# Hybrid conv, attention and MLP kernel: the token layer norms cut into four slices

## The chip, the cores and the metric

One core of a Trainium2 chip runs the whole kernel. The metric is the device time of one execution in microseconds (us), as the median of several runs.

## The reference, cut to what matters

The whole model has a Mamba stage over an image, a group norm with three depthwise convolutions, and then, for each of 4 batches of 4096 tokens with 96 channels, two layers of attention and MLP. The change lies in that last part alone:

```python
def _ln_t(v, eps=1e-5):
    m = jnp.mean(v, axis=-1, keepdims=True)
    s = jnp.var(v, axis=-1, keepdims=True)
    return (v - m) / jnp.sqrt(s + eps)
...
x = x + _L1_conv_ref(_gn(x), ...)
t = _to_tokens(x)
t = t + _L2_attn_ref(_ln_t(t), ...)      # linear attention, no softmax
t = t + _L2_ffn_ref(_ln_t(t), ...)       # 96 -> 384 -> 96, relu, fp8 products
t = t + _L3_attn_ref(_ln_t(t), ...)
t = t + _L3_ffn_ref(_ln_t(t), ...)
x = _from_tokens(t, x)
```

Every token's 96 values are normalised before each of the four blocks of a batch, 16 times in all over a tile of 4096 tokens.

## The kernel before, in words

The first 3.57 ms (the Mamba stage, the group norm and the depthwise convolutions) are not touched. What follows is `batch_phase`'s last block, from 3569 us of the span to its end at 4346 us.

Tokens stand as 32 tiles of 128 tokens on the 128 partitions with 96 values each, so that a whole batch is 3072 elements a partition. A **chunk** is 4 tiles (512 tokens); a phase has 8 chunks. The prologue fuses the convolution outputs of batches 0 and 1 in 8 **groups** of 1024 tokens: TensorE multiplies (`fuse`, L1253), VectorE adds the residual (`add_input`, L1511), TensorE transposes (`turn_rows`, L1262), ScalarE copies to `t_next` (`rows`, L1391). The groups of batches 2 and 3 are fused one or two at a time at the start of phases 1 to 7 (`FUSE_PHASE`); finished batches are transposed and stored ahead of phases 8 and 9 and after phase 15 (`turn_out`, L1350).

There are 16 **phases**, numbered p: attention of batch 0, attention of batch 1, MLP of batch 0, MLP of batch 1, the same for layer 2, and then all of it for batches 2 and 3. So phases 0, 1, 4, 5, 8, 9, 12 and 13 are attention, and 2, 3, 6, 7, 10, 11, 14 and 15 are MLP. The layer norm of phase p+1 is computed during phase p; that can be done because it needs the output of phase p-1. Each engine has its program in a fixed, hand-written order, and semaphores count what is done.

One **layer norm** is this chain. VectorE `center`: a sum over the 96 channels (L1487), a small multiply by 1/96 (L1488), a subtraction into `dev` (L1489). ScalarE `squares` (L1378): `dev` squared into `haug`. VectorE `variance`: a sum (L1495) and a small multiply-add (L1496). ScalarE `roots` (L1383). VectorE `scale`: a small reciprocal (L1501) and the product of `dev` and the reciprocal into `haug` (L1502). Each is one instruction over all 32 tiles. TensorE waits for the whole norm before its phase (`ln_ready`, p + 1).

An **attention phase**: TensorE transposes each chunk of `haug` (`turn`, L1272; ScalarE copies it to `h_t`, L1398) and adds its Gram matrix (L1286); when all 8 chunks are in, four small products follow one another (L1297), each with a VectorE instruction behind it (L1523 to L1531, the first being the copy of the Gram matrix); then the output products chunk by chunk (L1306), each added to the residual by VectorE (L1539). The two-slot PSUM tile `tp` holds transposes and outputs, so TensorE can be two chunks ahead of who empties them. VectorE's order is: `center`, `add_input` where a group is due, `variance`, the five Gram steps, `scale`, eight residual additions. ScalarE's is: `h_t` copies of chunks 0 to 5, `squares`, copies 6 and 7, `roots`.

An **MLP phase**, for each chunk and three thirds: TensorE multiplies (L1337), ScalarE evicts to `hid16` (L1431, four slots), VectorE adds a bias with relu (L1556) and casts to fp8 (L1550), TensorE multiplies back (L1320), ScalarE copies out (L1419), and GpSimd adds the bias (L1596) and then adds to the residual (L1599). VectorE does `center` after chunk 1, `variance` after chunk 4, `scale` after chunk 6; ScalarE does `squares` after chunk 3 and `roots` after chunk 5.

In the prologue VectorE does `center(0)` after group 3, `variance(0)` after group 4, `scale(0)` after group 5, and ScalarE does `squares(0)` and `roots(0)` between the copies of groups 3 and 4.

Of the kernel before, what the change touches and what calls it, by code (L numbers as in the profile page):

```python
# [11 lines left out]
ALU = mybir.AluOpType  # L12
# [830 lines left out]
CONV_GROUPS = 4  # L843
# [18 lines left out]
def batch_phase(nc, dram, f_dram, x0_dram, x_stats, f_stats, out):  # L862
# [4 lines left out]
    with ExitStack() as ctx:  # L867
# [352 lines left out]
        with nc.Block() as block:  # L1220
# [23 lines left out]
            def _(pe):  # L1244
# [21 lines left out]
                def turn(p, c, kind, rows):  # L1266

                    fill = fills[kind, p, c]
                    if fill >= 2:
                        pe.wait_ge(t_taken, fill - 1)  # L1270
                    for j in range(4):
                        last = pe.transpose(tp[0:rows, fill % 2, j * TILE:(j + 1) * TILE], haug[:, p % 2, 4 * c + j, 0:rows],  # L1272
                                            ident[:, :])
                    last.then_inc(t_full, 1)

                def attention(p):
                    n, layer = nth(p), phase_of(p)[1]
                    pe.wait_ge(ln_ready, p + 1)
                    pe.wait_ge(t_taken, fills[ATT_T, p, 0])
# [30 lines left out]
                def mlp(p):  # L1310
# [13 lines left out]

                    pe.wait_ge(ln_ready, p + 1)
                    pe.wait_ge(t_taken, fills[MLP_T, p, 0])
# [47 lines left out]
            def _(act):  # L1374
                def squares(v):

                    act.wait_ge(ln_centered, v + 1)
                    act.activation(haug[:, v % 2, :, 0:C], dev[:, :, :], ACT.Square).then_inc(ln_squared, 1)  # L1378

                def roots(v):  # L1380

                    act.wait_ge(ln_var, v + 1)
                    act.activation(stat[:, 2, :], stat[:, 1, :], ACT.Sqrt).then_inc(ln_root, 1)  # L1383

# [9 lines left out]
                def attention(p):  # L1394
                    for c in range(CHUNKS):
                        fill = fills[ATT_T, p, c]
                        act.wait_ge(t_full, fill + 1)
                        act.activation(h_t[:, c * CHUNK:(c + 1) * CHUNK], tp[0:C + 1, fill % 2, :],  # L1398
                                       ACT.Copy).then_inc(t_taken, 1)
                        if p + 1 < PHASES and c == SQUARE_AFTER[0]:  # L1400
                            squares(p + 1)
                    if p + 1 < PHASES:
                        roots(p + 1)

                def mlp(p):
# [17 lines left out]
                    for c in range(CHUNKS):  # L1423
# [8 lines left out]
                        if c > 0:  # L1432
                            add_up(c - 1)
                        if p + 1 < PHASES and c == SQUARE_AFTER[1]:
                            squares(p + 1)
                        if p + 1 < PHASES and c == ROOT_AFTER:
                            roots(p + 1)
                    add_up(CHUNKS - 1)
# [12 lines left out]
                squares(0)  # L1451
                roots(0)
                for i in range(CONV_GROUPS, first):
                    rows(i)
                for p in range(PHASES):
# [12 lines left out]
            def _(dve):  # L1468
# [7 lines left out]

                def center(v):

                    b, layer, is_mlp = phase_of(v)
                    src = residual_of(v)  # L1480
# [6 lines left out]
                    chain(dve.tensor_reduce(stat[:, 0, :], src, AXIS.X, ALU.add))  # L1487
                    chain(dve.tensor_scalar(stat[:, 0, :], stat[:, 0, :], 1.0 / C, None, ALU.mult))  # L1488
                    dve.tensor_tensor(dev[:, :, :], src, stat[:, 0, :].unsqueeze(2).to_broadcast([128, TILES, C]),  # L1489
                                      ALU.subtract).then_inc(ln_centered, 1)  # L1490

                def variance(v):

                    dve.wait_ge(ln_squared, v + 1)
                    chain(dve.tensor_reduce(stat[:, 1, :], haug[:, v % 2, :, 0:C], AXIS.X, ALU.add))  # L1495
                    dve.tensor_scalar(stat[:, 1, :], stat[:, 1, :], 1.0 / C, LN_EPS, ALU.mult, ALU.add).then_inc(ln_var, 1)  # L1496

                def scale(v):

                    dve.wait_ge(ln_root, v + 1)  # L1500
                    chain(dve.reciprocal(stat[:, 2, :], stat[:, 2, :]))  # L1501
                    dve.tensor_tensor(haug[:, v % 2, :, 0:C], dev[:, :, :], stat[:, 2, :].unsqueeze(2).to_broadcast([128, TILES, C]),  # L1502
                                      ALU.mult).then_inc(ln_ready, 1)

# [9 lines left out]
                def attention(p):  # L1514
                    n, (b, layer, _) = nth(p), phase_of(p)
                    if p + 1 < PHASES:
                        center(p + 1)
                    for i in due(FUSE_PHASE, p):
                        add_input(2 * CONV_GROUPS + i)
                    if p + 1 < PHASES:  # L1520
                        variance(p + 1)
                    dve.wait_ge(gram_full, n + 1)
# [8 lines left out]
                    dve.tensor_tensor(gram[:, 0, 0:C], mp[0:C + 1, 0, 0:C], bff[:, layer, :], ALU.add).then_inc(gram_step, 1)  # L1531
                    if p + 1 < PHASES:
                        scale(p + 1)
                    src = residual_of(p)
                    for c in range(CHUNKS):
# [3 lines left out]
                        dve.tensor_tensor(t[:, b % 2, tiles, :].rearrange("p j c -> p (j c)"), tp[:, fill % 2, 0:4 * C],  # L1539
                                          src[:, tiles, :].rearrange("p j c -> p (j c)"), ALU.add).then_inc(t_taken, 1)  # L1540

                def mlp(p):
# [9 lines left out]
                    for c in range(CHUNKS):  # L1552
# [20 lines left out]
                for i in range(CONV_GROUPS):  # L1573
# [126 lines left out]
```

## Time and profile before

| what | value |
|---|---|
| runs | 4346.25, 4350.67, 4351.54 us; median 4350.67 |
| profiled execution | 4347.45 us, of which the span of its instructions is 4345.6 us |
| mean granted TensorE clock | 0.918 of full speed |
| whole span, busy | TensorE 85%, VectorE 77%, GpSimd 66%, ScalarE 55% |
| prologue and phases | 3569 to 4346 us: 777 us, of which TensorE 527.5, VectorE 444.0, ScalarE 282.4, GpSimd 155.5 us busy |
| an attention phase | 33 to 47 us, by what is fused or stored in front of it |
| an MLP phase | 43 to 50 us; the last one, which has no layer norm to compute, 29 us |

The profile is one execution on the chip. A timeline row gives the start, the duration, the engine and line, the operation, the tiles with their sizes (partitions x elements), how many instructions the row holds, and in square brackets the idle time of that engine just before it and who ended it. "PE" is TensorE, "DVE" VectorE, "ACT" ScalarE, "POOL" GpSimd.

### The profile page before, as it was taken

To read this page: it belongs to the slowest core of one execution; us is meant where nothing else is said; L and a number is where in the kernel's file an instruction comes from. 1 tells how busy PE (TensorE), PEld (TensorE's weight loads), DVE (VectorE), ACT (ScalarE), POOL (GpSimd) and SP (SyncE) were. 2 spreads that over 40 slices of the span, in tenths; PEclk is the share of its full clock that TensorE was granted. 3 is DMA by queue.
4 is the path that set the end of the run, shared out by engine and by line. 5 is a ranking of instruction groups with operands and counts; after the bars stand their busy time and mean duration, and the time that the engine had idled before them with its cause. 6 is when DMAs were issued, how large, how long until landed. Compare 5 with 4: busy or idle time off the path is not lost. (4 is left out here: it accounts for less than half of the span.)

```text
span 4345.6 us, 39976 instructions
## 1 busy us (share of the span) xinstructions
PE 3674.2 (85%) x11136; PEld 1703.6 (39%) x11136; DVE 3347.4 (77%) x3962; ACT 2373.1 (55%) x3961; POOL 2852.7 (66%) x2326
## 2 busy tenths in 40 slices
PE   6899999999999999999999999987129988685766
PEld 2333333333333333333333333332029985463554
DVE  4999999999999999999999999999320004656565
ACT  5667666667666667666667666665121101425334
POOL 4988999988999988999988999988100000203123
PEclk8999999999999999999999999999569998777666
DMA  3555555555555555555555555555564456100000
GB/s 89 180 160 166 164 166 162 175 169 165 164 165 162 177 168 164 168 161 162 178 168 163 168 162 163 175 160 170 134 163 145 147 146 154 31 15 15 15 1 29
DMA packets 246461, 607.50 MB, mean 140 GB/s; under 512 B 56496, under 2 KB 90419, under 8 KB 245087
## 3 DMA queue, kind: packets, MB, share of 16 engines
q1 hardware_dynamic: 210654, 535.73, 41.9%
q10 hardware_dynamic: 35584, 69.23, 5.7%
q8 instruction: 89, 1.46, 0.1%
q14 instruction: 134, 1.09, 0.1%
HBM read 553.77 MB, written 72.56 MB: 144 GB/s over the span
## 5 line engine op out<-in xcount | busy, mean ns | idle before, releaser
L785 POOL TENSOR_TENSOR prod<-states,c_rows 128x512 f32<-128x512 f32 x1536 | 1922.7, 1272 | 176.9 <-DVE states L715 142.7
L715 DVE TENSOR_TENSOR_SCAN states<-decay,carry,bpsum 128x512 f32<-128x512 f32 x1344 | 1677.2, 1259 | 0.0
L444 PE MATMUL ypsum<-prod,identity 128*128 128x512 f32 x3072 | 1593.7, 602 | 0.5 <-POOL prod L785 0.3
L550 ACT ACTIVATE decay<-delta,decay_rate 128x512 f32<-128x512 f32 x1344 | 934.7, 711 | 312.5 <-DVE states L715 308.2
L695 DVE TENSOR_TENSOR bpsum<-bpsum,dx 128x512 f32<-128x512 f32 x1344 | 904.6, 673 | 138.5 <-PE bpsum L437 124.3
L1596 POOL TENSOR_TENSOR y<-y,b 128x384 f16<-128x384 f16 x64 | 66.4, 1038 | 1072.3 <-ACT y L1419 1072.3
L444 PEld LDWEIGHTS ypsum<-prod,identity 128*128 128x128 f32 x3072 | 583.3, 194 | 422.4 <-issue 283.4
L437 PE MATMUL bpsum<-b_rows,select 96*128 96x512 bf16 x1344 | 522.0, 389 | 211.8 <-DVE states L715 209.3
L437 PEld LDWEIGHTS bpsum<-b_rows,select 96*128 96x128 bf16 x1344 | 129.4, 96 | 974.3 <-DVE states L715 690.7
L1020 PE MATMUL convp<-image,band_w 128*128 128x252 f32 (+3 forms) x1440 | 334.2, 395 | 19.2 <-DMA image<-normed_map 19.2
L1020 PEld LDWEIGHTS convp<-image,band_w 128*128 128x128 f32 x1440 | 332.7, 325 | 20.4 <-issue 19.2
L550 ACT ACTIVATE bpsum<-delta,decay_rate 128x512 f32<-128x512 f32 x192 | 132.6, 691 | 309.6 <-DVE states L715 308.7
L1572 DVE MEMSET haug<- 128x64 f32 x1 | 0.1, 112 | 356.6 <-PEq L1151 356.6
L484 PE MATMUL mm<-h_norm,w_xs 96*128 96x512 f32 x512 | 262.7, 599 | 6.0 <-ACT h_norm L616 6.0
L492 PE MATMUL mm<-h_norm,w_xs 96*64 96x512 f32 x512 | 267.5, 616 | 0.0
L813 POOL TENSOR_TENSOR drive<-b_wide,dx 128x512 f32<-128x512 f32 x192 | 243.9, 1270 | 30.1 <-DMA b_wide<-bc_map 28.5
L715 DVE TENSOR_TENSOR_SCAN states<-bpsum,carry,drive 128x512 f32<-128x512 f32 x192 | 243.7, 1269 | 0.9 <-issue 0.9
L626 ACT ACTIVATE xpre<-mm,cols 128x512 f32<-128x512 f32 x96 | 65.7, 684 | 301.2 <-PE mm L492 168.6
L794 POOL TENSOR_TENSOR tmp<-zpre,tmp 128x512 f32<-128x512 f32 x96 | 122.3, 1274 | 130.3 <-ACT zpre L595 130.3
L1064 ACT ACTIVATE dw_sums<-convp 128x768 f32<-128x768 f32 x48 | 38.9, 811 | 307.4 <-PE convp L1020 307.4
L1556 DVE TENSOR_SCALAR hid<-hid,b 128x512 f16<-128x512 f16 x192 | 90.3, 488 | 88.7 <-ACT hid L1431 84.3
L484 PEld LDWEIGHTS mm<-h_norm,w_xs 96*128 96x128 f32 x512 | 97.9, 192 | 132.3 <-issue 123.7
(184 smaller groups left out, 4486.3 us busy)
## 6 DMA issues: line engine op xcount, KB each, us to landing
c_rows<-bc_map SPq DMA_DIRECT2D x512, 512.0 KB, 3.9
c_rows<-bc_map SPq DMA_DIRECT2D x512, 256.0 KB, 4.1
b_wide<-bc_map ACTq DMA_DIRECT2D x128, 256.0 KB, 4.7
band_rows<-tap_bands SPq DMA_DIRECT2D x64, 360.0 KB, 5.6
band_w<-band_rows SPq DMA_DIRECT2D x96, 240.0 KB, 3.9
depthwise_map<-dw_sums ACTq DMA_DIRECT2D x48, 384.0 KB, 4.4
dw_parts<-depthwise_map SPq DMA_DIRECT2D x16, 1152.0 KB, 7.7
b_wide<-bc_map ACTq DMA_DIRECT2D x128, 128.0 KB, 4.2
```

Source lines behind the costliest of these rows:

```text
L437: pe.matmul(bpsum[:, n % B_BANKS, :], pick, b_rows[k % 2][:, :], start=True, stop=True).then_inc(b_full, 1)
L444: pe.matmul(ypsum[:, group % Y_BANKS, :], identity[:, :], prod[:, n % P_RING, :], start=s == 0, stop=s == STATES - 1).then_inc(summed, 1)
L484: last = pe.matmul(mm[:, b, :], w_xs[:, layer, k, 0:128], h_norm[:, b, k:k + CHUNK], start=k == 0, stop=k == TAPS - 1)
L492: last = pe.matmul(mm[b * HALF:b * HALF + HALF, 0, :], w_xs[:, layer, k, 128:DIN], h_norm[:, b, k:k + CHUNK], start=k == 0, stop=k == TAPS ...
L550: act.activation(into, delta[k % 2][:, g, :], ACT.Exp, scale=decay_rate[:, ORDER[k][0], g, s:s + 1]).then_inc(done, 1)
L695: dve.tensor_tensor(bpsum[:, n % B_BANKS, :], bpsum[:, n % B_BANKS, :], dx[k % 2][:, g, :], ALU.mult).then_inc(scaled, 1)
L715: dve.tensor_tensor_scan(states[:, n % H_RING, :], by, add, carry[:, at, u:u + 1], ALU.mult, ALU.add).then_inc(scanned, 1)
L785: pool.tensor_tensor(prod[:, n % P_RING, :], states[:, n % H_RING, :], c_rows[:, n // C_STATES % C_RING, n % C_STATES, :], ALU.mult).then_ ...
L794: pool.tensor_tensor(tmp1[:, g, :], zpre[:, g, :], tmp1[:, g, :], ALU.subtract).then_inc(lost_ready, 1)
L813: pool.tensor_tensor(drive[:, i % B_RING, :], b_wide[:, i % B_RING, :], dx[k % 2][:, g, :], ALU.mult).then_inc(driven, 1)
L1020: last = pe.matmul(into[:, :, left:right], bands[:, p % W_RING, :, TAP_AT[k] + kx], image[:, p % I_RING, :, left + kx - pad:right + kx - pad],
L1556: dve.tensor_scalar(hid16[:, i % 4, :], hid16[:, i % 4, :], b1[:, layer, k:k + 1], 0.0, ALU.add, ALU.max).then_inc(hid_relu, 1)
```

## The change

Each norm is cut into `SLICES` = 4 slices of 8 tiles (768 elements a partition), and every step of the chain is issued once for a slice. The semaphores count slices (`SLICES * v + k + 1`), also where TensorE waits: `turn` of chunk c waits for slice c // 2 alone. `center` waits for the two chunks (or the one group) that its slice reads, and no more for all of them.

- Prologue: `center(0, k)` stands after group k + 2, `variance(0, k)` after k + 4, `scale(0, k)` after k + 5; ScalarE squares after copies 3 to 6 and takes roots after copies 4 to 7.
- Attention: VectorE does four `center` slices, `add_input`, four `variance` slices, the Gram steps, and `scale(k)` behind the residual additions 1, 3, 5 and 7. ScalarE does `squares(k)` behind the `h_t` copies 1, 3, 5 and 7, and the four roots at the end.
- MLP: `center(k)` after chunk k, `squares(k)` in chunk k + 1, `variance(k)` after chunk k + 2, `roots(k)` in chunk k + 3, `scale(k)` after chunk k + 4.

```diff
-SQUARE_AFTER, ROOT_AFTER = (5, 3), 5
-CENTER_AFTER, VARIANCE_AFTER, SCALE_AFTER = 1, 4, 6
+SLICES = 4
+ATT_SQUARE, ATT_SCALE = (1, 3, 5, 7), (1, 3, 5, 7)
+MLP_CENTER, MLP_SQUARE, MLP_VARIANCE, MLP_ROOT, MLP_SCALE = range(5)
+SLICE = TILES // SLICES
...
                 def turn(p, c, kind, rows):
+                    pe.wait_ge(ln_ready, SLICES * p + c * SLICES // CHUNKS + 1)
...
-                    pe.wait_ge(ln_ready, p + 1)
...
-                def squares(v):
-                    act.wait_ge(ln_centered, v + 1)
-                    act.activation(haug[:, v % 2, :, 0:C], dev[:, :, :], ACT.Square).then_inc(ln_squared, 1)
+                def squares(v, k):
+                    act.wait_ge(ln_centered, SLICES * v + k + 1)
+                    tiles = slice(SLICE * k, SLICE * (k + 1))
+                    act.activation(haug[:, v % 2, tiles, 0:C], dev[:, tiles, :], ACT.Square).then_inc(ln_squared, 1)
...
                 def center(v, k):
                     b, layer, is_mlp = phase_of(v)
+                    tiles = slice(SLICE * k, SLICE * (k + 1))
                     if layer == 0 and not is_mlp:
-                        dve.wait_ge(rows_taken, CONV_GROUPS * (b + 1))
+                        dve.wait_ge(rows_taken, CONV_GROUPS * b + k + 1)
                     elif not is_mlp:
-                        dve.wait_ge(t_step, CHUNKS * (nth(v - 2) + 1))
+                        dve.wait_ge(t_step, CHUNKS * nth(v - 2) + CHUNKS // SLICES * (k + 1))
                     else:
-                        dve.wait_ge(t_taken, fills[ATT_O, v - 2, CHUNKS - 1] + 1)
+                        dve.wait_ge(t_taken, fills[ATT_O, v - 2, CHUNKS // SLICES * (k + 1) - 1] + 1)
...
                 def attention(p):
-                        center(p + 1)
+                        for k in range(SLICES):
+                            center(p + 1, k)
...
-                        variance(p + 1)
+                        for k in range(SLICES):
+                            variance(p + 1, k)
...
-                    if p + 1 < PHASES:
-                        scale(p + 1)
...
+                        if p + 1 < PHASES:
+                            for k in due(ATT_SCALE, c):
+                                scale(p + 1, k)
...
                 def mlp(p):
-                            if c == CENTER_AFTER:
-                                center(p + 1)
-                            if c == VARIANCE_AFTER:
-                                variance(p + 1)
-                            if c == SCALE_AFTER:
-                                scale(p + 1)
+                            if 0 <= c - MLP_CENTER < SLICES:
+                                center(p + 1, c - MLP_CENTER)
+                            if 0 <= c - MLP_VARIANCE < SLICES:
+                                variance(p + 1, c - MLP_VARIANCE)
+                            if 0 <= c - MLP_SCALE < SLICES:
+                                scale(p + 1, c - MLP_SCALE)
...
-                for i in range(CONV_GROUPS):
-                    add_input(i)
-                center(0)
-                add_input(CONV_GROUPS)
-                variance(0)
-                add_input(CONV_GROUPS + 1)
-                scale(0)
-                for i in range(CONV_GROUPS + 2, 2 * CONV_GROUPS):
-                    add_input(i)
+                for i in range(2 * CONV_GROUPS + 1):
+                    if i < 2 * CONV_GROUPS:
+                        add_input(i)
+                    if 0 <= i - 2 < SLICES:
+                        center(0, i - 2)
+                    if 0 <= i - 4 < SLICES:
+                        variance(0, i - 4)
+                    if 0 <= i - 5 < SLICES:
+                        scale(0, i - 5)
```

## Rows read from the trace of the kernel before

**Rows 1.** Busy us by window, phase 15: PE, PEld, DVE, ACT, POOL, then clock

```profile
4291.00:4320.00 29.00, 18.21 (x149) 11.41 (x150) 23.01 (x48) 20.34 (x39) 16.44 (x16) 0.85 0.00 1
```

**Rows 2.** Groups by line and form, 3564 to 4346 us: busy us, mean ns, idle before

```profile
L1502 DVE TENSOR_TENSOR haug<-dev_t,stat 128x3072 f32<-128x3072 f32 x16 | 57.1, 3572 | 0.5
L1495 DVE TENSOR_REDUCE stat<-haug 128x32 f32<-128x3072 f32 x16 | 53.6, 3350 | 66.3 <-ACT haug L1378 66.3
...
L1378 ACT ACTIVATE haug<-dev_t 128x3072 f32<-128x3072 f32 x16 | 44.1, 2759 | 8.5 <-DVE dev_t L1489 8.5
L1489 DVE TENSOR_TENSOR dev_t<-t,stat 128x3072 f32<-128x3072 f32 x12 | 40.3, 3358 | 0.4
...
L1511 DVE SCALAR_TENSOR_TENSOR x<-convp,vecs,x_group 96x1024 f32<-96x1024 f32 x16 | 20.4, 1278 | 46.0 <-PE convp L1253 46.0
...
L1539 DVE TENSOR_TENSOR t<-tp,t 128x384 f32<-128x384 f32 x32 | 17.4, 556 | 29.6 <-PE tp L1306 29.6
...
L1501 DVE RECIPROCAL stat<-stat 128x32 f32<-128x32 f32 x16 | 5.5, 342 | 0.0
```

**Rows 3.** Timeline of the prologue: TensorE's products of groups 4, 5 and 6

```profile
3605.81 5.39 PE L1253 MATMUL convp<-dw_parts,wf 96*96 96x512 f32 x12 [0.90 <-ACT t_next L1391]
...
3612.76 5.39 PE L1253 MATMUL convp<-dw_parts,wf 96*96 96x512 f32 x12 [0.90 <-ACT t_next L1391]
...
3627.13 8.27 PE L1253 MATMUL convp<-dw_parts,wf 96*96 96x512 f32 x12 [5.30 <-ACT t_next L1391]
```

**Rows 4.** Timeline of attention phase 1

```profile
3685.95 0.60 PE L1272 MATMUL tp<-ident,haug 128*97 128x128 f32 x4
...
3687.07 0.60 PE L1272 MATMUL tp<-ident,haug 128*97 128x128 f32 x4
...
3695.49 3.35 DVE L1495 TENSOR_REDUCE stat<-haug 128x32 f32<-128x3072 f32 x1 [8.06 <-ACT haug L1378]
...
3698.97 0.25 DVE L1523 COPY gram<-mp 97x97 f32<-97x97 f32 x1
...
3703.22 3.73 PE L1306 MATMUL tp<-gram,h_t 97*128 97x96 f32 x16 [0.35 <-DVE gram L1531]
...
3707.34 10.56 PE L1306 MATMUL tp<-gram,h_t 97*128 97x96 f32 x48 [0.39 <-DVE t L1539]
```

**Rows 5.** Timeline of attention phases 12 and 13

```profile
4179.00 1.14 PE L1272 MATMUL tp<-ident,haug 128*97 128x128 f32 x4 [0.63 <-issue]
...
4180.92 3.35 DVE L1487 TENSOR_REDUCE stat<-t 128x32 f32<-128x3072 f32 x1 [3.81 <-POOL t L1599]
...
4194.19 0.25 DVE L1523 COPY gram<-mp 97x97 f32<-97x97 f32 x1
...
4213.82 1.14 PE L1272 MATMUL tp<-ident,haug 128*97 128x128 f32 x4 [0.70 <-issue]
...
4228.24 0.26 DVE L1523 COPY gram<-mp 97x97 f32<-97x97 f32 x1
```

**Rows 6.** Timeline of MLP phase 10

```profile
4095.95 0.84 DVE L1556 TENSOR_SCALAR hid<-hid,b 128x512 f16<-128x512 f16 x2 [3.16 <-ACT hid L1431]
...
4108.13 0.61 DVE L1556 TENSOR_SCALAR hid<-hid,b 128x512 f16<-128x512 f16 x2
...
4109.93 0.61 DVE L1556 TENSOR_SCALAR hid<-hid,b 128x512 f16<-128x512 f16 x2
...
4112.87 0.91 POOL L1599 TENSOR_TENSOR t<-t,y 128x384 f32<-128x384 f32 x1
...
4115.45 0.84 DVE L1556 TENSOR_SCALAR hid<-hid,b 128x512 f16<-128x512 f16 x2 [3.65 <-ACT hid L1431]
...
4121.16 1.27 DVE L1556 TENSOR_SCALAR hid<-hid,b 128x512 f16<-128x512 f16 x2
...
4130.27 1.92 DVE L1556 TENSOR_SCALAR hid<-hid,b 128x512 f16<-128x512 f16 x2
...
4133.36 0.75 DVE L1550 CAST hid<-hid 128x512 fp8e5<-128x512 f16 x2
```

More of the change, by code:

```diff
@@ L1399, in attention @@
                                        ACT.Copy).then_inc(t_taken, 1)
-                        if p + 1 < PHASES and c == SQUARE_AFTER[0]:
-                            squares(p + 1)
+                        if p + 1 < PHASES:
+                            for k in due(ATT_SQUARE, c):
+                                squares(p + 1, k)
                     if p + 1 < PHASES:
-                        roots(p + 1)
+                        for k in range(SLICES):
+                            roots(p + 1, k)
                 def mlp(p):
@@ L1433, in mlp @@
                             add_up(c - 1)
[L1434 to L1437, printed above, removed]
+                        if p + 1 < PHASES:
+                            if 0 <= c - MLP_SQUARE < SLICES:
+                                squares(p + 1, c - MLP_SQUARE)
+                            if 0 <= c - MLP_ROOT < SLICES:
+                                roots(p + 1, c - MLP_ROOT)
                     add_up(CHUNKS - 1)
@@ L1448, in _ @@
                 first = 2 * CONV_GROUPS
-                for i in range(CONV_GROUPS):
+                for i in range(first):
                     rows(i)
[L1451 to L1454, printed above, removed]
+                    if 0 <= i - 3 < SLICES:
+                        squares(0, i - 3)
+                    if 0 <= i - 4 < SLICES:
+                        roots(0, i - 4)
                 for p in range(PHASES):
@@ L1475, in chain, with center @@
                     dve.wait_ge(dve_step, count[0])
-                def center(v):
+                def center(v, k):
                     b, layer, is_mlp = phase_of(v)
-                    src = residual_of(v)
+                    tiles = slice(SLICE * k, SLICE * (k + 1))
+                    src = residual_of(v)[:, tiles, :]
                     if layer == 0 and not is_mlp:
-                        dve.wait_ge(rows_taken, CONV_GROUPS * (b + 1))
+                        dve.wait_ge(rows_taken, CONV_GROUPS * b + k + 1)
@@ L1490, in center @@
+                    chain(dve.tensor_reduce(stat[:, 0, tiles], src, AXIS.X, ALU.add))
+                    chain(dve.tensor_scalar(stat[:, 0, tiles], stat[:, 0, tiles], 1.0 / C, None, ALU.mult))
+                    dve.tensor_tensor(dev[:, tiles, :], src, stat[:, 0, tiles].unsqueeze(2).to_broadcast([128, SLICE, C]),
                                       ALU.subtract).then_inc(ln_centered, 1)
[L1492 to L1503, printed above, removed]
+                def variance(v, k):
+                    tiles = slice(SLICE * k, SLICE * (k + 1))
+                    dve.wait_ge(ln_squared, SLICES * v + k + 1)
+                    chain(dve.tensor_reduce(stat[:, 1, tiles], haug[:, v % 2, tiles, 0:C], AXIS.X, ALU.add))
+                    dve.tensor_scalar(stat[:, 1, tiles], stat[:, 1, tiles], 1.0 / C, LN_EPS, ALU.mult, ALU.add).then_inc(ln_var, 1)
@@ L1505, in add_input, with scale @@
+                def scale(v, k):
+                    tiles = slice(SLICE * k, SLICE * (k + 1))
+                    dve.wait_ge(ln_root, SLICES * v + k + 1)
+                    chain(dve.reciprocal(stat[:, 2, tiles], stat[:, 2, tiles]))
+                    dve.tensor_tensor(haug[:, v % 2, tiles, 0:C], dev[:, tiles, :],
+                                      stat[:, 2, tiles].unsqueeze(2).to_broadcast([128, SLICE, C]), ALU.mult).then_inc(ln_ready, 1)
                 def add_input(i):
@@ L1520, in attention @@
                     if p + 1 < PHASES:
-                        variance(p + 1)
+                        for k in range(SLICES):
+                            variance(p + 1, k)
                     dve.wait_ge(gram_full, n + 1)
@@ L1540, in attention @@
                                           src[:, tiles, :].rearrange("p j c -> p (j c)"), ALU.add).then_inc(t_taken, 1)
+                        if p + 1 < PHASES:
+                            for k in due(ATT_SCALE, c):
+                                scale(p + 1, k)
                 def mlp(p):
```

12 lines of the change are left out of this document (4 added, 8 removed).

## The prediction

> **What bounds the kernel now.** Only the prologue and the 16 phases can change; the 3569 us before them stay. I read three views: the busy time by window for where VectorE fills its time, the groups by line for what a norm costs, and the timeline for what TensorE waits for. The last MLP phase, which computes no norm, takes 29 us [rows 1]; the other seven take 43 or more, so a norm costs an MLP phase about 14 us. A norm on VectorE is a sum of 3.35, a subtraction of 3.36, another sum of 3.35 and a product of 3.57 us, with ScalarE's square of 2.76 us between, for which VectorE waited 66.3 us in all [rows 2]. So it is hardly hidden: VectorE or the chain through it is the bound in every stage.
>
> **Prices of a slice.** The subtraction takes 3.36 us for 3072 elements and the residual addition 0.556 us for 384 [rows 2]: 1.04 ns an element and 0.156 us fixed. A slice of 768 then costs 0.96 us. Bounds: a plain quarter, 0.84 us, and 1.01 us with the fixed 0.21 us that the addition of 1024 elements (1.278 us) leaves at that slope [rows 2]. I take 0.96, the row of the same operation. The reciprocal is near 0.20 and the small multiply near 0.17 us, estimates from 0.34 us for a reciprocal of 32 elements [rows 2] and the fixed 0.156. With 0.04 us for each hand-over and 0.09 us by which the next instruction overlaps, a slice is 2.06 us of `center`, 1.07 of `variance`, 1.10 of `scale`: 16.9 us a norm against 14.1 in one piece. ScalarE's square of a slice is near 0.8 us (a quarter is 0.69).
>
> What the rows of VectorE give is also what a page says. By the Trainium skill ("VectorE: DVE Perf Modes", the section on the TRN2 errata) every VectorE instruction pays a fixed latency, (N+151)/0.96 ns for an fp32 two-tensor operation, so that many small tiles pay it each. That gives 0.957 us for a slice, the same price, and speaks against the change; how much of it reaches the path is a rival below.
>
> **Prologue.** Groups start 6.95 us apart (3605.81, 3612.76), but group 6 starts at 3627.13 instead of 3619.71, 7.42 us late, since its slot waits for ScalarE's copy behind the square and the root of norm 0; and it ran 8.27 us instead of 5.39, 2.88 more, at the lower clock after TensorE's pause [rows 3]. After the change the fullest slot holds one addition (1.28), one `center`, one `variance` and one `scale`: 5.5 us, under 6.95. ScalarE's waits lie a slot behind. Both losses go: **-10.3 us** (bounds -7.4, if the clock falls anyway, and -10.3).
>
> **Attention.** The Gram copy, from which the small products and the outputs follow, stands on VectorE behind `variance`. In phase 1 it comes at 3698.97, 13.0 us after the first transpose (3685.95), since the sum waited 8.06 us for the square, which ScalarE does behind copy 5 [rows 4]. TensorE turns a chunk every 1.12 us (3685.95, 3687.07 [rows 4]), so that all is in at about 9.2 us, and copy c of ScalarE starts at 0.6 + 1.12 c. Now three squares are done by then; the last one follows copy 7, at 9.1 to 9.9 us, and its `variance` ends at 11.0: 2.0 us gained. Where a fusion or stores come first (phases 1, 4, 5, 8, 9) VectorE's four `center` slices and the `scale(3)` before them, 9.3 us, are done in time. In phase 12 VectorE now need not wait for GpSimd's last addition (3.81 us idle, copy at 15.2 us [rows 5]); there the limit is again copy 7, at 10.7 us as TensorE starts slowly, so the copy comes at 12.6: 2.6 gained. In phase 13 nothing covers `center`: `scale(3)` ends at 1.0, the centres at 9.3, the variances at 13.5 us, against 14.4 [rows 5]: 0.9 gained. Phase 0 is as phase 13, but VectorE is still in norm 0 until 3.8 us: centres end at 12.1, variances at 16.4, against 14.4: 2.0 lost, with ScalarE's copies held up behind squares that wait, at no cost to the end. Then the outputs: the third chunk started 4.12 us after the first (3703.22, 3707.34 [rows 4]) where two chunks take 3.42, because `scale` stood before the additions; now it stands between them (0.56 + 1.10 us in 3.42): 0.7 gained in each of 8. Sum: 5 x 2.7 + 3.3 + 1.6 - 1.3 = **-17.1 us** (bounds -25, if the last variance overlaps more, and -5, if the squares cost the copies).
>
> **MLP.** From the first relu at 4095.95 to the end of the last cast at 4134.11 phase 10 takes 38.2 us [rows 6]. It holds 8 chunks of 1.80 us of relu and cast (4108.13 to 4109.93), the norm's 14.1, a wait of 3.65 us while ScalarE squares (4115.45) [rows 6], and some 4.6 us in which VectorE is held up by GpSimd: two relus take 0.60 alone, 1.27 when GpSimd's pair is running and 1.92 when GpSimd had waited through the product; GpSimd's addition alone takes 0.91 [rows 6]. Sums don't collide with it, subtractions, products, relus and casts do. After: 8 x 1.80 + 0.5 for the start; in the window 4 `center`, 4 `variance` and 3 `scale` (the fourth falls behind the last cast, where VectorE waits for the next phase anyway): 15.8. The square's wait goes, since ScalarE squares a slice two chunks ahead. Without GpSimd that is 30.7 us. But VectorE is now busy throughout, and GpSimd's pair for chunk c starts some 1.8 us after the casts of chunk c, inside the subtraction, and takes its turn at the relus of c+1. I walk it: 1.3 us after chunks 0, 1 and 6; 0.6 after 2 and 3, where its first half lies under the variance's sum; 1.3 after 4 and 5: 7.7 us, against 4.6. So 38.4 against 38.2. In phases 2, 3, 6 and 7 an addition of 1.28 us [rows 2] that fell into waiting time is now on the path: +1.0 each. Together **+5 us** (3 x 0.2 + 4 x 1.0, rounded). Bounds: at the old 4.6 us of collisions the seven gain 3 each, -18; at 0.9 us for each of 14 GpSimd additions the window is 43.3, +38.
>
> No DMA, no queue and no step of SP is moved; group loads keep ahead of the groups at 6.95 us, as they do for groups 2 to 5.
>
> **Sum.** -10.3 - 17.1 + 5 = -22.4 us. The profiled execution took 4347.45 us, 3.2 under the median of 4350.67; the sum is taken from either alike, and from the median it gives **4328 us**. A measurement of this kernel can tell about 0.2%, 8.7 us, from no change.
>
> **Rivals.**
> - *GpSimd collides no more than before.* For it: a sum is still 8 of 36 us, and the pairs may fall into sums. Against: their start is tied to the casts, and the sum is over by then. MLP -18 instead of +5: 4305 us. 20%.
> - *VectorE is full and the attention gain shrinks*, because the squares hold up the copies and the last variance comes as late as before. Attention only gains the 5.6 us of the outputs, MLP +5: 4340 to 4345 us. 17%.
> - *Slower: GpSimd's port in the MLP.* Place: the seven MLP windows. Each of the 14 additions holds VectorE for its 0.9 us [rows 6]: +38 in place of +5, 4361 us. The gain is gone once collisions pass 10.9 us a phase (7.7 + 22.4/7). For: the row of 1.92 us. Against: in the last phase, where VectorE is as full (23.0 of 29 us [rows 1]), relus and casts take 8 x 1.80 plus 8.6 us at most. 6%.
> - *The fixed costs all land on the path.* Slicing adds 21 VectorE instructions of 0.156 us a norm; if nothing hides them, the attention phases lose 3.3 where they gain 0.7, the MLP phases stay, the prologue gains: 4350.7 - 10.3 + 8 x 2.6 + 5 = 4366 us. 4%. By the rule of the Trainium skill named above, with its 0.157 us an instruction, the price is the same; the page asks for operations of at least 512 elements, which these are.
> - *The semaphore counts leave a wait as it was*, so that only the prologue moves: 4340 us. 3%.
>
> **How the numbers follow.** My case has 50%, from 4315 to 4340. Range: from 4303, which takes in most of the first rival, to 4349, leaving out the two slow cases and some of the fast tail. Chances: faster by over 0.2% (below 4342): 0.50 + 0.20 + half of the second and the last, 0.10, less 0.02 for my own case's tail: 0.78. Within 0.2%: 0.14. Slower: 0.08.
>
> **What would show it.** Group 6 starts near 3619.7 at 5.39 us; the first transpose of phase 0 near 3634. The Gram copy of phases 1, 4, 5, 8 and 9 comes 11 us after the first transpose; of phase 0, 16. The outputs of an attention phase run without the 0.39 us wait. No relu waits for ScalarE over 1 us in an MLP phase, and VectorE's busy share there passes 90%; relus and casts take longer in sum than now. The forecast is wrong if the window from first relu to last cast leaves 36 to 41 us, or if a sliced instruction is off 0.84 to 1.01 us.

## The result, and the profile after

The changed kernel takes 4326.55 us (median of 4 runs, 4324.68 to 4326.91); the kernel before took 4350.77 beside it (4 runs). The ratio is 0.9946, interval 0.9928 to 0.9963: faster by 24 us. The profiled execution took 4326.91 us with a span of 4325.1, against a span of 4345.6 before: 20.5 us less. That is what the traces can place; the other 3.7 us between the medians lie within the spread of single executions.

The page of the changed kernel, its first lines:

```profile
span 4325.1 us, 40519 instructions
...
PE 3699.6 (86%) x11136; PEld 1712.0 (40%) x11136; DVE 3413.3 (79%) x4298; ACT 2384.9 (55%) x4057; POOL 2826.6 (65%) x2326
```

VectorE is busy 65.9 us longer (3347.4 before) with 336 more instructions, 16 x 21, and the kernel is faster. What it gained was waiting time, as the groups by line show (line, engine, operation, out<-in; then busy us, mean ns, idle us before and its releaser), for the stretch from 3545 us on:

```profile
L1511 DVE TENSOR_TENSOR haug<-dev_t,stat 128x768 f32<-128x768 f32 x64 | 61.3, 958 | 2.2
L1503 DVE TENSOR_REDUCE stat<-haug 128x8 f32<-128x768 f32 x64 | 60.6, 947 | 35.3 <-ACT haug L1380 35.3
...
L1380 ACT ACTIVATE haug<-dev_t 128x768 f32<-128x768 f32 x64 | 53.7, 839 | 20.4 <-DVE dev_t L1496 20.4
L1496 DVE TENSOR_TENSOR dev_t<-t,stat 128x768 f32<-128x768 f32 x48 | 46.0, 959 | 1.6
...
L1504 DVE TENSOR_SCALAR stat<-stat 128x8 f32<-128x8 f32 x64 | 21.1, 330 | 2.2
...
L1510 DVE RECIPROCAL stat<-stat 128x8 f32<-128x8 f32 x64 | 12.3, 193 | 0.0
```

Beside [rows 2]: a slice of the subtraction or the product costs 0.96 us, the second sum waits 35.3 us for the square instead of 66.3, and the small operations stand near 0.17 and 0.19 us (the 330 ns of L1504 hold waits for GpSimd, below).

The prologue, TensorE's products of groups 4 to 7 and the first transpose of phase 0, where [rows 3] had 7.4 us of delay and a slow group:

```profile
3605.25 5.39 PE L1255 MATMUL convp<-dw_parts,wf 96*96 96x512 f32 x12 [0.90 <-ACT t_next L1394]
...
3612.20 5.39 PE L1255 MATMUL convp<-dw_parts,wf 96*96 96x512 f32 x12 [0.90 <-ACT t_next L1394]
...
3619.15 5.39 PE L1255 MATMUL convp<-dw_parts,wf 96*96 96x512 f32 x12 [0.90 <-ACT t_next L1394]
...
3626.10 5.39 PE L1255 MATMUL convp<-dw_parts,wf 96*96 96x512 f32 x12 [0.90 <-ACT t_next L1394]
...
3633.58 0.60 PE L1275 MATMUL tp<-ident,haug 128*97 128x128 f32 x4
```

Attention phase 1, for [rows 4]:

```profile
3674.25 0.60 PE L1275 MATMUL tp<-ident,haug 128*97 128x128 f32 x4
...
3683.25 0.83 ACT L1380 ACTIVATE haug<-dev_t 128x768 f32<-128x768 f32 x1
3684.11 0.95 DVE L1503 TENSOR_REDUCE stat<-haug 128x8 f32<-128x768 f32 x1 [1.09 <-ACT haug L1380]
...
3685.18 0.25 DVE L1534 COPY gram<-mp 97x97 f32<-97x97 f32 x1
3685.49 0.41 PE L1299 MATMUL mp<-wv,gram 97*97 97x96 f32 x2 [2.09 <-DVE gram L1534]
...
3688.60 13.97 PE L1308 MATMUL tp<-gram,h_t 97*128 97x96 f32 x64 [0.35 <-DVE gram L1542]
```

The Gram copy comes 10.93 us after the first transpose (13.02 before). The outputs run in one piece. TensorE's pause in front of the four small products is 2.09 us, and three of them take 0.41 us and the last 0.48, at a granted clock of 0.91 for 3685.4 to 3688.5 us; in the kernel before the pause was 4.18 us, and all took 0.64 at a clock of 0.50, the lower level of 1.2 GHz.

MLP phase 10 of the changed kernel, from its first relu to its last cast, for [rows 6]:

```profile
4076.19 0.84 DVE L1568 TENSOR_SCALAR hid<-hid,b 128x512 f16<-128x512 f16 x2 [2.04 <-ACT hid L1436]
...
4080.12 1.22 POOL L1608 TENSOR_TENSOR y<-y,b 128x384 f16<-128x384 f16 x1 [89.82 <-ACT y L1424]
4080.48 2.00 DVE L1568 TENSOR_SCALAR hid<-hid,b 128x512 f16<-128x512 f16 x2
4081.42 0.91 POOL L1611 TENSOR_TENSOR t<-t,y 128x384 f32<-128x384 f32 x1
...
4091.90 0.91 POOL L1611 TENSOR_TENSOR t<-t,y 128x384 f32<-128x384 f32 x1
4091.95 0.89 DVE L1504 TENSOR_SCALAR stat<-stat 128x8 f32<-128x8 f32 x1
...
4113.79 1.46 DVE L1562 CAST hid<-hid 128x512 fp8e5<-128x512 f16 x2
```

Behind the first, no relu waits for ScalarE here for more than 0.14 us any more (3.65 us before), and VectorE is busy 98% of the window instead of 88%, yet the window is 39.06 us, where it was 38.16. Two relus beside GpSimd's pair take 2.00 us instead of 0.60, and a small multiply 0.89 instead of 0.17. Such excess stands in the phase 8.4 us long: 1.4 five times (the last in two parts) and 0.72 twice.

Stage by stage, both traces laid side by side:

| part | before to after, us | predicted |
|---|---|---|
| prologue, to the first transpose | -10.3, and 0.6 from an earlier start | -10.3 |
| attention, first transpose to Gram copy, 8 phases | -12.0 | -11.5 |
| attention, Gram copy to outputs | -3.2 (34.0 to 30.8) | 0 |
| attention, outputs, 14.68 to 13.97 | -5.7 | -5.6 |
| MLP windows, first relu to last cast, 7 with a norm | +8.4 | +5 |
| what lies between, and the stores at the end | about +3 | 0 |

### The profile page after: what moved, and what is told of

Same layout as the page of the kernel before. It is cut to its first block and busy times, and to the rows that moved or that the text cites. A ratio compares the mean times of both kernels' runs of the same rounds, so it can differ in the third digit from the quotient of the medians.

```text
span 4325.1 us, 40519 instructions
## 1 busy us (share of the span) xinstructions
PE 3699.6 (86%) x11136; PEld 1712.0 (40%) x11136; DVE 3413.3 (79%) x4298; ACT 2384.9 (55%) x4057; POOL 2826.6 (65%) x2326
## 5 line engine op out<-in xcount | busy, mean ns | idle before, releaser
L1338 PE MATMUL mp<-h,w 96*128 96x512 fp8e5 x192 | 91.7, 538 | 74.4 <-ACT hid L1436 73.3
```

## The experiments

Every ratio below is to runs of the kernel before on the same chip, whose medians were 4346.5 to 4347.5 us. Beside the changed kernel that median was 4350.8, so a difference from the changed kernel comes out up to 4 us apart by times and by ratios; where that matters, stretches of the traces decide. The two kernels with small GpSimd additions were run once each, the others four to ten times.

**The prologue: order or waits?** Norm 0's slices back at the old places, still sliced:

```diff
-                    if 0 <= i - 2 < SLICES:
-                        center(0, i - 2)
-                    if 0 <= i - 4 < SLICES:
-                        variance(0, i - 4)
-                    if 0 <= i - 5 < SLICES:
-                        scale(0, i - 5)
+                    for k in range(SLICES):
+                        if i == 3:
+                            center(0, k)
+                        if i == 4:
+                            variance(0, k)
+                        if i == 5:
+                            scale(0, k)
```

(on ScalarE the four squares and the four roots behind copy 3)

> The changed kernel with norm 0 put back to its old places in the prologue (all four center slices after group 3, variance after group 4, scale after group 5, squares and roots between copies 3 and 4), still in slices. My theory is that the prologue's gain of 10.3 us comes from the places: then group 6 starts late again behind the square and the root, the clock falls and group 6 runs near 8.3 us, and the time is 4337 to 4340 us (10.3 us back, and 1 to 3 for the fixed cost of the slices, which is now in the path). Rival: the hand-over slice by slice is what helps, wherever the slices stand; then it stays under 4332 us.

Measured: 4325.94 us, ratio 0.9953 (0.9938 to 0.9968), the time of the changed kernel. The rival was right. Then the same with the norm in one piece, one instruction of 3072 elements for each step with its wait for all four groups, and nothing else changed:

```diff
-                    if 0 <= i - 2 < SLICES:
-                        center(0, i - 2)
+                    if i == 3:
+                        mean(0, 0, SLICES)
+                        deviate(0, 0, SLICES)
```

(`mean` and `deviate` are the two halves of `center`; variance and scale likewise behind 4 and 5, the square and the root behind copy 3)

> The changed kernel with norm 0 alone in one piece and in its old places, waiting for all four groups and handing on whole. If it is the fine waits that made the prologue faster, group 6 starts 7.4 us late again and runs at 8.3 us, so that the first transpose of phase 0 comes 10.3 us later than in the changed kernel; phase 0 then gets its Gram copy some 4 us earlier, as in the first experiment, since norm 0 is out of the way: 4331 to 4333 us. Rival: the time stays within 2 us of 4325, and the prologue's gain has another source.

Measured: 4333.32 us, ratio 0.9969 (0.9957 to 0.9981), 0.3 us above what was expected. The first sum of the norm and group 6 in the two, the sliced one first:

```profile
3603.97 0.94 DVE L1495 TENSOR_REDUCE stat<-t_next 128x8 f32<-128x768 f32 x1
...
3619.81 5.39 PE L1255 MATMUL convp<-dw_parts,wf 96*96 96x512 f32 x12 [2.51 <-ACT t_next L1394]
```

```profile
3612.09 3.35 DVE L1493 TENSOR_REDUCE stat<-t_next 128x32 f32<-128x3072 f32 x1 [7.17 <-ACT t_next L1394]
...
3626.75 8.68 PE L1255 MATMUL convp<-dw_parts,wf 96*96 96x512 f32 x12 [4.84 <-ACT t_next L1394]
```

At the old places, sliced, the sums and subtractions of groups 0 to 2 run while group 3 is on its way, and group 6 is 1.6 us late at most. The whole norm waits 7.17 us for the copy of group 3. Counted from the start of group 5 in each kernel (3611.24 and 3612.11 us), its last subtraction ends 4.9 us later than in slices, and the copy that group 6 waits for ends 6.1 us later; the 1.2 us between come from the square, for which VectorE waits 1.72 us when it is whole and not at all in slices. So most of the old loss went because a slice waits for its own group. No run cuts the norm and lets every slice wait for all four groups, so the 4.9 us rest on these rows. Spreading the slices over seven places added 1.6 us to that. The old order paid that back in phase 0, whose Gram copy came 11.63 us after the first transpose instead of 15.94 (the fuse behind it then took 1.1 us longer). The whole norm has that too, which is why its span is only 7.4 us longer than the changed kernel's, although its first transpose comes 10.9 us later (3644.47 us).

**Attention: what the places are worth.** The four squares together behind copy 5 and the four products ahead of the residual additions, as the whole norm had them:

```diff
-ATT_SQUARE, ATT_SCALE = (1, 3, 5, 7), (1, 3, 5, 7)
+ATT_SQUARE, ATT_SCALE = (5, 5, 5, 5), (1, 3, 5, 7)
...
+                    if p + 1 < PHASES:
+                        for k in range(SLICES):
+                            scale(p + 1, k)
...
-                        if p + 1 < PHASES:
-                            for k in due(ATT_SCALE, c):
-                                scale(p + 1, k)
```

> The changed kernel with the old order in the attention phases, in slices: the four squares all behind copy 5, the four scale slices between the Gram steps and the residual additions. The four squares then end 10.0 us after the first transpose where the last of them ended at 9.9, with the variances piped behind them, so I expect the Gram copy where it is in the changed kernel (10.9 us), and only the outputs to lose, 0.7 us for the wait that comes back and 0.7 for four scales in place of one: 4337 us. Rival: it is the squares' places that brought the Gram copy from 13.0 to 10.9 us; then 12 us more are lost, 4349 us.

Measured: 4348.59 us, ratio 1.0004 (0.9995 to 1.0014): the whole gain of the change is gone. Its phase 1:

```profile
3684.44 0.95 DVE L1503 TENSOR_REDUCE stat<-haug 128x8 f32<-128x768 f32 x1 [5.21 <-ACT haug L1380]
...
3688.69 0.25 DVE L1534 COPY gram<-mp 97x97 f32<-97x97 f32 x1
...
3689.00 0.64 PE L1299 MATMUL mp<-wv,gram 97*97 97x96 f32 x2 [3.02 <-DVE gram L1534]
...
3697.84 10.55 PE L1308 MATMUL tp<-gram,h_t 97*128 97x96 f32 x48 [1.16 <-DVE t L1551]
```

In this phase the Gram copy is 11.86 us after the first transpose (3676.83 us), 0.93 late: my expectation said 0, the rival 2.1, and both were off. The small products are at 0.64 us again, behind a pause of 3.02 us, and the outputs wait 1.16 us for additions that stand behind four products. Summed over the eight phases, the copies come 5.3 us later, the small products take 2.6 us more and the outputs 11.8 (15.44 us each for 13.97): 19.7 us, of the 19.8 by which the span is longer than the changed kernel's. So the larger part is the place of the products, not of the squares, and the rival's 4349 us was met by another sum than its own. Then the other way, the last square behind copy 5 instead of 7:

```diff
-ATT_SQUARE, ATT_SCALE = (1, 3, 5, 7), (1, 3, 5, 7)
+ATT_SQUARE, ATT_SCALE = (1, 3, 5, 5), (1, 3, 5, 7)
```

> The changed kernel with the attention squares behind copies 1, 3, 5 and 5 in place of 1, 3, 5 and 7. If the last square, and through it the last variance, sets the Gram copy in the phases that begin behind fusions or stores, the copy comes at 9.6 to 9.9 us after the first transpose in place of 10.9 and five to six phases gain 1 to 1.3 us: 4319 to 4322 us. Rival: VectorE's own order, with center before it, or the Gram matrix itself sets it; then 4326 us, unchanged.

Measured: 4318.70 us, ratio 0.9934 (0.9918 to 0.9951). In phase 1 the copy comes at 9.75 us instead of 10.93:

```profile
3676.61 0.60 PE L1275 MATMUL tp<-ident,haug 128*97 128x128 f32 x4
...
3683.36 1.57 ACT L1380 ACTIVATE haug<-dev_t 128x768 f32<-128x768 f32 x2
...
3686.36 0.25 DVE L1534 COPY gram<-mp 97x97 f32<-97x97 f32 x1
3686.67 0.41 PE L1299 MATMUL mp<-wv,gram 97*97 97x96 f32 x2 [0.90 <-DVE gram L1534]
```

So in this phase the last square is the limit, as the prediction had it. In phases 0 and 13, where the slices of `center` themselves are late, it moved nothing (15.94 and 13.45).

**MLP: slices against whole, and GpSimd.** First the norms of the MLP phases whole again, at their old places:

```diff
-                            if 0 <= c - MLP_CENTER < SLICES:
-                                center(p + 1, c - MLP_CENTER)
+                            if c == 1:
+                                center(p + 1, SLICES)
```

(`SLICES` as the slice number stands for the whole norm here; `variance` behind chunk 4, `scale` behind 6, ScalarE as before the change; the attention phases keep their slices)

> The changed kernel with the norms that are computed during MLP phases in one piece and in their old places; prologue and attention phases stay sliced. The windows from first relu to last cast grew by 1.4 us in phases 2, 3, 6 and 7 and by 0.9 in 10, 11 and 14, so if slicing is a loss there the time falls by about 8 us: 4318 us, with windows of 38.1 us. Rival: the slices pay in some other place (the start of the phase behind, GpSimd's lag), and the time is 4325 us or more.

Measured: 4318.35 us, ratio 0.9936 (0.9921 to 0.9951), windows of 37.6 to 39.0 us: slicing the norm in the MLP phases cost 8 us by the times and 7.1 us in the seven windows (4 us by the ratios). Next, GpSimd's two additions for a chunk cut to one of the 96 channels, in both kernels; this leaves out the bias and the residual addition of the other 95 channels in the MLP phases.

```diff
-                            pool.tensor_tensor(y, y, b2[:, layer, :, :], ALU.add).then_inc(y_biased, 1)
+                            pool.tensor_tensor(y[:, :, 0:1], y[:, :, 0:1], b2[:, layer, :, 0:1], ALU.add).then_inc(y_biased, 1)
...
-                            pool.tensor_tensor(t[:, b % 2, tiles, :], t[:, b % 2, tiles, :], y, ALU.add).then_inc(t_step, 1)
+                            pool.tensor_tensor(t[:, b % 2, tiles, 0:1], t[:, b % 2, tiles, 0:1], y[:, :, 0:1], ALU.add).then_inc(t_step, 1)
```

> The kernel before, with GpSimd's two additions of the MLP phases done on 1 of the 96 channels: it leaves out the MLP's bias and residual in the other 95. With next to nothing left of GpSimd's hold on the port, the window from first relu to last cast shrinks by what I put down to collisions: 4.6 us in phases with a norm (38.1 to 33.5), about 6 in the last. Rival: the waits are not GpSimd's; then the windows stay at 38.

> The changed kernel with the same thin additions, which leave out the same part. In its phase 10 the drawn-out relus, casts and small multiplies add up to 8.4 us, so the window should fall from 39.1 to near 31 us (39.5 to near 31.5 with a group to add), and be shorter than the old kernel's 33.5 with thin additions: without GpSimd slicing would be a gain of over 2 us a phase. Rival: the slices' fixed cost is what made the windows longer; then this kernel stays at least 1 us above the old one's thin window.

Measured: spans of 4308.6 and 4263.4 us. The kernel before loses 4.0 to 4.3 us a window (to 34.0 and 33.9), the changed one 7.8 and 8.4 (to 31.7 and 30.7). Phase 10 of the changed kernel with the small additions, where the relus of the second chunk and the small multiply are back at the times they take alone, 0.61 and 0.17 us (2.00 and 0.89 above):

```profile
4044.12 0.84 DVE L1568 TENSOR_SCALAR hid<-hid,b 128x512 f16<-128x512 f16 x2 [2.04 <-ACT hid L1436]
...
4048.43 0.61 DVE L1568 TENSOR_SCALAR hid<-hid,b 128x512 f16<-128x512 f16 x2
...
4057.12 0.17 DVE L1504 TENSOR_SCALAR stat<-stat 128x8 f32<-128x8 f32 x1
```

Without GpSimd's work, then, slicing is a gain of 2.4 to 3.2 us a phase, and GpSimd takes 8 of it back where it took 4 before. Between four slices and one lie two, with each sum set where a pair is likely to come (behind the subtraction of the other slice):

```diff
-                            if 0 <= c - MLP_CENTER < SLICES:
-                                center(p + 1, c - MLP_CENTER)
-                            if 0 <= c - MLP_VARIANCE < SLICES:
-                                variance(p + 1, c - MLP_VARIANCE)
-                            if 0 <= c - MLP_SCALE < SLICES:
-                                scale(p + 1, c - MLP_SCALE)
+                            if c == 0:
+                                mean(p + 1, 0, 2)
+                            if c == 1:
+                                deviate(p + 1, 0, 2)
+                                mean(p + 1, 2, 2)
+                            if c == 2:
+                                deviate(p + 1, 2, 2)
+                                variance(p + 1, 0, 2)
+                            if c == 4:
+                                scale(p + 1, 0, 2)
+                                variance(p + 1, 2, 2)
+                            if c == 6:
+                                scale(p + 1, 2, 2)
```

(ScalarE squares the two slices in chunks 2 and 3 and takes their roots in chunks 3 and 5)

> The changed kernel with the norms of the MLP phases in two slices of 16 tiles, placed so that a sum of 1.8 us stands behind a subtraction or product in chunks 1, 2 and 4, under GpSimd's pair, which starts 1.8 us after the casts. If sums cover the pair, three of seven collisions of 1.4 us go and the fixed cost falls by 1 us: windows of 36 to 37 us, 4306 to 4312 us. Rival: the pair finds the port busy wherever it stands, and only the fixed cost is saved: 4319 to 4323 us.

Measured: 4298.08 us, ratio 0.9887 (0.9870 to 0.9903), windows of 35.3 to 35.7 us, under both theories' numbers. And the same with each sum directly ahead of its own subtraction:

```diff
-                            if c == 0:
-                                mean(p + 1, 0, 2)
                             if c == 1:
+                                mean(p + 1, 0, 2)
                                 deviate(p + 1, 0, 2)
-                                mean(p + 1, 2, 2)
                             if c == 2:
+                                mean(p + 1, 2, 2)
                                 deviate(p + 1, 2, 2)
```

> The version with two slices of 16 tiles in the MLP phases (4298.1 us, windows 35.3 to 35.7), but with the sum of a slice directly ahead of its subtraction, in chunks 1 and 2, in place of one chunk or half a chunk ahead. Width and number of instructions are the same; only which VectorE instruction meets GpSimd's pair differs. Theory, by collisions: the subtractions of chunks 1 and 2 meet a pair each, 1.4 us each, 2.8 us a phase, windows 38.1 to 38.5 and 4314 to 4322 us. Rival, that the gain came from half the fixed costs and fewer waits alone: windows 35.3 to 36.2 and 4298 to 4303 us.

Measured: 4305.95 us, ratio 0.9902 (0.9887 to 0.9916), windows of 36.0 to 37.0: my theory, with 38.1 to 38.5, was wrong, the rival nearer (its time, 4298 to 4303, was missed too). Its phase 10:

```profile
4076.52 1.76 DVE L1501 TENSOR_TENSOR dev_t<-t,stat 128x1536 f32<-128x1536 f32 x1
4077.53 1.53 POOL L1623 TENSOR_TENSOR y<-y,b 128x384 f16<-128x384 f16 x1 [6.39 <-ACT y L1424]
4078.20 1.75 DVE L1512 TENSOR_REDUCE stat<-haug 128x16 f32<-128x1536 f32 x1
4079.14 0.91 POOL L1626 TENSOR_TENSOR t<-t,y 128x384 f32<-128x384 f32 x1
...
4083.88 0.91 POOL L1623 TENSOR_TENSOR y<-y,b 128x384 f16<-128x384 f16 x1 [3.83 <-ACT y L1424]
4084.12 2.29 DVE L1520 TENSOR_TENSOR haug<-dev_t,stat 128x1536 f32<-128x1536 f32 x1
4084.87 2.31 POOL L1626 TENSOR_TENSOR t<-t,y 128x384 f32<-128x384 f32 x1
4086.33 1.74 DVE L1512 TENSOR_REDUCE stat<-haug 128x16 f32<-128x1536 f32 x1
```

Whoever starts first holds the other off. GpSimd's addition at 4077.53 came under the subtraction, which began 1.01 us before it: the subtraction took the 1.76 us that it takes alone, and the addition 1.53 us for 0.91. The next addition lay under the sum, and both took their own time. The product at 4084.12 began inside GpSimd's addition of 4083.88 and paid 0.53 us for it (2.29 for 1.76); GpSimd's second addition, at 4084.87, then waited for the product and took 2.31 us, ending in the sum behind it, which paid nothing. So a pair costs VectorE 0.53 us there and not 1.4: its second half drifts into the sum, if one stands there. The Trainium skill ("SBUF — State Buffer", the section "Who interferes with whom") has both sides as a rule: the port pair that VectorE and GpSimd share is held by one instruction at a time, whoever starts first, and a sum (tensor_reduce) never needs it. The rows agree on the sums and on the two directions.

The excess of VectorE's instructions over their times alone, summed over phase 10, is 8.4 us with four slices, 5.7 here and 5.2 with the sums spread; its windows of 39.06, 36.48 and 35.33 us less that are 30.7, 30.8 and 30.2, and with GpSimd's work gone the one of four slices was 30.7. So between four slices and two most of the difference in the window is collisions. As these rows read, the number of slices enters mainly through how many instructions meet GpSimd's; that is not shown by a run, since the kernels of two slices were not run without its work.

**Together.** Two slices in the MLP phases and (1, 3, 5, 5) in the attention phases:

> Two slices of 16 tiles in the MLP phases and the last square one chunk earlier in the attention phases, together. The two alone stood 28 us (4298.1) and 7 us (4318.7; by its span 4 us) below the changed kernel. They work in different phases, so my theory says that the gains add: 4291 to 4295 us. A rival: the shorter MLP windows leave TensorE at a lower granted clock in the attention phases or in the fusing groups between them, and part of the 4 to 7 us is lost: 4296 to 4299.

Measured: 4287.34 us, ratio 0.9860 (0.9845 to 0.9874), below the 4291 to 4295 of my theory; the gains of the two alone, added by their ratios, give 0.9875, which is not clear of this one with the noise of three ratios. In phases 1, 4 and 5 the outputs start 13.08 us after the first transpose: 9.75 to the copy and 3.33 for all four small products at 0.41 us each. The outputs behind them take 13.40, 12.92 and 13.69 us, where they took 13.97. The rival had the sign wrong: TensorE's granted clock was higher here, not lower (0.922 over the whole run, 0.916 with the early square alone). With norm 0's slices at the old places too:

> As the run before, with the first norm's slices at their old places in the prologue too, which alone was worth 0.6 us (4325.9 for 4326.6): phase 0's Gram copy comes 4.3 us earlier, and about 1.7 us of it is lost before phase 0 and 1.1 behind it. Theory: 0 to 2 us below the run before. Rival, if what is gained in phase 0 is given back in full by the fuse behind it: no difference, or 1 us more.

Measured: 4285.90 us, ratio 0.9856 (0.9839 to 0.9872), not to be told from the last, so neither theory is decided. Its group 6 is again 1.6 us late, and this time the group itself ran slow:

```profile
3621.77 8.55 PE L1255 MATMUL convp<-dw_parts,wf 96*96 96x512 f32 x12 [2.51 <-ACT t_next L1394]
```

The same pause of 2.51 us cost nothing in the first experiment and 3.2 us here (a granted clock of 1.00 in that group there, 0.62 here).

## Why the prediction was right, point by point

The forecast of 4328 us lay 1.5 us above the median, and its case was the right one: prologue and attention gain, the MLP phases lose a little.

- **Price of a slice.** 0.96 us predicted, 958 and 959 ns measured; reciprocal 0.193 for 0.20, small multiply 0.17, square 0.839 for "near 0.8". (Of a slice's seven instructions four have 768 elements and three have 8, so the 512 that the forecast took as met are met by four.) The Trainium skill's rule ("VectorE: DVE Perf Modes", the TRN2 errata section) gives 0.957 us, and the trace agrees. The fixed costs are there (65.9 us of VectorE more, the collisions among them), but in the attention phases they went into waits, and the rival of 4366 us was far off.
- **Prologue, -10.3.** Right to 0.1 us, with group 6 on time and at 5.39 us. The reason was only partly right. I gave it to the slots that the slices are spread over. The runs show that places are worth 1.6 us before phase 0 and nothing in the time of the kernel, and that the rest comes from the cut itself, most of it from slices that wait for one group (4325.94 sliced and 4333.32 whole, at the same places).
- **Attention, -17.1.** It was -20.9. Gram copies: 2.1 to 2.3 us for the 2.0 of the common case, 1.9 for 2.6 in phase 12, 1.0 for 0.9 in phase 13, 1.6 lost for 2.0 in phase 0; outputs 0.71 for 0.7. One of my signs did not come: in phases 8 and 9 the copy stands 12.35 and 13.44 us after the first transpose and not 11. The gain was right there because the copies before were late too (14.58 and 15.70), which the prediction had not read. The term left out is the clock of the small products: behind the shorter pause 12 of the 32 took 0.41 us, where all had taken 0.64, and their stretches are 3.2 us shorter in the eight phases, of which nothing stood in the sum.
- **MLP, +5.** It was +8.4. The mechanism held and its size was a little off: collisions of 8.4 us for 7.7 in phase 10, windows of 39.06 for 38.4. Work without GpSimd was put at 30.7 us, and the run with small additions gave 30.7. The rival of 4305 us, that GpSimd collides no more than before, fell; so did the slower one, whose 10.9 us of collisions a phase were not reached. (By its own working the bounds of this term are -16 and +40, not -18 and +38; the two rivals that use them move by 2 us.)
- **Costed at nothing.** What lies between the stages, the fuse steps and the stores at the end, took about 3 us more. Between phases 2 and 3 a group is fused in 7.45 us instead of 5.94 (row below; the granted clock in it is 0.71, before 0.90), and from the last cast to the end it is 28.2 us instead of 26.4. Why the clock stays low for longer there was not tried.
- Two misses nearly cancel (-3.8 in attention, +3.4 in the MLP). With the 3 us costed at nothing and the earlier start the traces give -20.5 for the forecast -22.4, and the medians differ by 24.2. That the forecast came within 1.5 us of the median owes something to chance.

The fused group of the fifth point, in the timeline of the changed kernel:

```profile
3755.37 7.45 PE L1255 MATMUL convp<-dw_parts,wf 96*96 96x512 f32 x12
```

## What to carry to other kernels

Cut an operation where that lets it wait for less, and set each piece behind the last thing it needs: in the attention phases the order of the slices is worth the whole gain, and more than half of that is the products that no longer stand ahead of the additions. The cut without a new order paid in the prologue alone; in the MLP phases four slices lost to one. Before cutting work on a VectorE that shares its time with GpSimd, count which instructions meet GpSimd's, and put sums there: two slices with well placed sums beat both one and four (4298 us, for 4318 and 4327). With the earlier square as well the kernel stands at 4287 us, 37 us faster than the change by the two ratios (0.9860 and 0.9946).

## What the runs showed of the hardware

- GpSimd's addition of 384 elements (0.91 us) draws 0.65 to 0.73 us from a VectorE relu, cast or small multiply that meets it, and 0.5 to 0.7 from a subtraction or product that begins while it runs. From a sum it draws nothing: a sum of 768 elements takes 0.94 us beside it and alone, and no sum in any of the traces was longer for it. Even an instruction of 8 elements pays in full (0.89 us for 0.17).
- The one that starts first pays nothing: a subtraction of 1536 elements kept its 1.76 us while GpSimd's addition that came into it took 1.53 us for 0.91, and behind a product of that size the addition took 2.31.
- Equal pauses of TensorE, 2.51 us in the same place, left the granted clock at 1.00 in one run and took it to 0.62 in another.
- Of the 32 small products of a kernel, none took 0.41 us behind pauses of 4.18 us and more (kernel before, clock 0.50 from the first of them; 2 with GpSimd's additions made small), 3 behind 3.02 (old order in attention), 12 behind 2.09 (changed kernel), 18 behind 0.90 (early square) and 27 behind 0.90 again, with two slices in the MLP phases besides; these are the pauses of most phases, and those of phases 0 and 13 are longer. The same pause of 2.09 us had three at 0.41 in phase 1 and two at 0.41 and two at 0.64 in phase 12. Other kernels here with the 2.09 us had 8 to 17. A shorter pause made the higher clock likelier and assured it nowhere, and the last two counts differ at one pause, so the pause alone does not set it.
